# Splits of the first quad and of wo's first data moved ahead, and ScalarE's order within a slot changed

## The reference

```python
# cond: linear layer plus a low-rank adapter chosen per sequence
base_out = jnp.einsum('bti,oi->bto', x, W) + b
lora_h = jnp.einsum('bti,bir->btr', x, lora_As[adapter_mapping])
c = base_out + jnp.einsum('btr,bro->bto', lora_h, lora_Bs[adapter_mapping]) * 2.0
# attention: 32 query heads on 8 key/value heads of 128, rotary positions, causal
q, k, v = _rope(c @ wq), _rope(c @ wk), c @ wv
attn = softmax(where(allowed, q @ k.T * sm_scale, neg))
x1 = x + (attn @ v) @ wo
# cond2: linear layer plus rank-16 experts, two best of 8 by router logits with a language bias
# ffn: linear layer plus rank-64 experts, two best of 16 by a softmax router; float32 output
```

## Time and profile before

| what | value |
|---|---|
| median of 3 runs | 2829.83 us (2829.41 to 2833.12) |
| the profiled execution's own time | 2826.46 us |
| its span in the profile | 2824.5 us |
| PE busy | 2701.7 us, 96% |
| POOL busy | 1198.7 us, 42% |
| DVE busy | 1344.0 us, 48% |
| ACT busy | 854.5 us, 30% |
| mean granted clock of PE | 0.986 |

### The profile page before, as it was taken

One profiled execution on the slowest core, in us unless ns is written; L12 is line 12 of the kernel. 1 busy time (PEld: TensorE's weight loads), 2 busy tenths in 40 slices (PEclk: granted clock), 3 DMA queues, 4 the chain that ended last, 5 costly groups with the idle time before them and its releaser, 6 DMA issues.

```text
span 2824.5 us, 37498 instructions
## 1 busy us (share of the span) xinstructions
PE 2701.7 (96%) x14520; PEld 2174.1 (77%) x14520; DVE 1344.0 (48%) x2011; ACT 854.5 (30%) x2089; POOL 1198.7 (42%) x790
## 2 busy tenths in 40 slices
PE   8979899999998999999998989999999899999999
PEld 7857677777776788887877767777777678888877
DVE  2124667777775111124533557777777511112452
ACT  2222244444443312221212224444444331121110
POOL 0025665655665245510304476566555434441020
PEclk9999999999999999999999989999999999999999
DMA  6853122222225333111543312222222433311322
GB/s 217 243 145 119 45 68 73 70 75 68 71 62 189 126 113 105 51 39 54 145 124 100 109 45 76 75 74 63 67 75 72 168 127 112 105 53 38 84 86 70
DMA packets 311984, 268.47 MB, mean 95 GB/s; under 512 B 68218, under 2 KB 283386, under 8 KB 311810
## 3 DMA queue, kind: packets, MB, share of 16 engines
q1 hardware_dynamic: 250210, 210.50, 24.6%
q10 hardware_dynamic: 61600, 55.58, 6.0%
HBM read 201.88 MB, written 64.16 MB: 94 GB/s over the span
## 4 chain that ended last, share of the span: by engine, by line
PE 85%; POOL 6%; ACT 3%; DMA 2%; issue 2%; SPq 1%; DVE 1%; ACTq 0%; POOLq 0%
PE prod L658 25%; PE prod L660 24%; PE prod L659 24%; PE turned L901 3%; PE turned L851 2%; POOL s_lo L1465 2%; POOL o_lo L1499 1%; ACT probs L1227 1%; ACT s_hi L1213 1%; PE turned L652 1%; PE turned L884 1%; PE prod L1086 1%; POOL w_sum L1489 1%; PE prod L766 1%; POOL w_lo L1430 1%
## 5 line engine op out<-in xcount | busy, mean ns | idle before, releaser
L1430 POOL TENSOR_TENSOR w_lo<-raw,w_hi 128x1024 fp32r<-128x1024 f32 x96 | 239.2, 2493 | 850.0 <-ACT w_hi L1146 728.0
L658 PE MATMUL prod<-o_hi,w_hi 128*128 128x512 f32 x1024 | 405.4, 396 | 22.9 <-POOL o_lo L1499 19.2
L659 PE MATMUL prod<-o_lo,w_hi 128*128 128x512 f32 x1024 | 400.8, 391 | 0.0
L660 PE MATMUL prod<-o_hi,w_lo 128*128 128x512 f32 x1024 | 400.4, 391 | 0.0
L1784 DVE TENSOR_TENSOR x<-prod,x 128x512 f32<-128x512 f32 x128 | 88.5, 692 | 603.3 <-PE prod L660 603.3
L1465 POOL TENSOR_TENSOR s_lo<-w_sum,s_hi 128x512 fp32r<-128x512 f32 x192 | 253.0, 1318 | 155.7 <-ACT s_hi L1213 155.7
L658 PE MATMUL prod<-t_hi,s_hi 128*128 128x512 f32 x768 | 312.2, 407 | 3.9 <-POOL s_lo L1465 3.9
L1146 ACT CAST w_hi<-raw 128x1024 fp32r<-128x1024 f32 x128 | 134.1, 1048 | 599.7 <-PE prod L660 428.0
L660 PE MATMUL prod<-t_hi,s_lo 128*128 128x512 f32 x768 | 300.5, 391 | 0.0
L659 PE MATMUL prod<-t_lo,s_hi 128*128 128x512 f32 x768 | 299.8, 390 | 0.0
L658 PE MATMUL prod<-b_hi,s_hi 128*128 128x512 f32 x576 | 239.9, 417 | 15.7 <-POOL s_lo L1465 15.7
(11 more groups left out here) (168 smaller groups left out, 5063.5 us busy)
## 6 DMA issues: line engine op xcount, KB each, us to landing
raw_pair<-in_wq SPq DMA_DIRECT2D x64, 512.0 KB, 4.7
o_scratch<-o_out ACTq DMA_DIRECT2D x64, 512.0 KB, 2.9
raw<-in_wo SPq DMA_DIRECT2D x64, 512.0 KB, 4.0
o_raw<-o_scratch SPq DMA_DIRECT2D x64, 512.0 KB, 7.2
raw<-t_scratch SPq DMA_DIRECT2D x50, 512.0 KB, 3.6
t_scratch<-x ACTq DMA_DIRECT2D x17, 512.0 KB, 4.2
x_raw<-in_x SPq DMA_DIRECT2D x16, 512.0 KB, 5.9
xt_scratch<-x_sum SPq DMA_DIRECT2D x16, 512.0 KB, 3.2
```

The lines of the kernel that those rows point to most:

```text
L658: pe.matmul(dst, wh, xh, start=start, stop=False)
L659: pe.matmul(dst, wh, xl, start=False, stop=False)
L660: return pe.matmul(dst, wl, xh, start=False, stop=stop)
L1430: pool.tensor_tensor(WL[i % 2][:], RAW[i % 2][:], WH[i % 2][:].bitcast(F32), ALU.subtract).then_inc(w_lo, 1)
```

## The change

Several instructions are moved; the arithmetic is the same.

1. `load_a1` of the first half is issued in the fold, ahead of the load for step 6, into a buffer of its own. On ACT and DVE the adapters' cast and subtraction stand behind those of the last four x blocks. For the second half SP issues the adapters behind the loads of W1 tiles 0 and 1; ACT casts tile 0 before the last early x block.
2. ACT casts W1 tile 2 once `h0`, the adapter product, is done, not once `c0` is.
3. `load_pair` loads each quad in two halves with a semaphore each. The first half may land when the last block sum of the quad before is made, the second when its last but one split is. For the first quad of each half of the tokens the halves follow the last two W1 tiles, and ACT casts its first two blocks before the last column of the first layer.
4. In each slot ACT does the attention work first and the cast for the next quad second. PE's second turn of probabilities and its copy on ACT move from slot 0 to slot 1.
5. In the last quad ACT casts wo's tiles 0 and 1 and the first eight pieces of o. POOL subtracts both tiles first, then twelve pieces; DVE subtracts the other four. The mask and exponentials of the tail stand one product earlier.

```diff
+                if i == 6:
+
+                    sp.wait_ge(const_in, 16 * 5)
+                    sp.wait_ge(fold_taken, 4)
+                    load_a1(0)
...
+                for h in range(2):
+                    ks = slice(4 * h, 4 * h + 4)
+                    if g == 0 and qd == 0:
+                        sp.wait_ge(w_lo, pool_no(hf, T_WO - 2 + h) + 1)
+                    elif h == 0:
+                        sp.wait_ge(s_sum, 4 * (n - 1) + 4)
+                    else:
+                        sp.wait_ge(s_lo, 7 * (n - 1) + 6)
...
-                                if at_ == (QD_KV, 0):
+                                if at_ == (QD_KV, 1):
                                     turn_p(gg - 1, 0, 1)
-                                if at_ == (QD_KV, 1):
                                     score(gg - 1, 1, 0)
...
+                for b in range(4, TB):
+                    x_hi(hf, b)
                 act.wait_ge(a_in, 16 * TT * SPT * (hf + 1))
...
-                act.copy(AH[:], AW[:]).then_inc(a_hi, 1)
-                for b in range(4, TB):
-                    x_hi(hf, b)
+                act.copy(AH[:], AWS[hf][:]).then_inc(a_hi, 1)
...
-                for n in range(KC):
+
+                tile_hi(hf, 2, QN["h0"])
+                c_hi(0)
+                for n in range(1, KC):
                     c_hi(n)
                     tile_hi(hf, n + 2, QN[f"c{n}.0"])
...
+                    if j == 3:
+                        s_high(pair_no(hf, 0, 0), 0)
+                        s_high(pair_no(hf, 0, 0), 1)
...
-                            if more and i == 4:
-                                s_high(n + 1, 4)
-                                s_high(n + 1, 3)
-                            elif more and i != 3:
-                                s_high(n + 1, i)
...
+                            if more and i == 4:
+                                s_high(n + 1, 4)
+                                s_high(n + 1, 3)
+                            elif more and i != 3:
+                                s_high(n + 1, i)
+                            if not more:
+
+
+                                if i == 2:
+                                    act.wait_ge(qprod, q_done(last, 1))
+                                    tile_hi(hf, T_WO)
+                                if i == 3:
+                                    act.wait_ge(qprod, q_done(last, 3))
+                                    tile_hi(hf, T_WO + 1)
+                                if i in (5, 6):
+                                    for c in range(4 * (i - 5), 4 * (i - 5) + 4):
+                                        o_high(0, c)
...
                 tile_lo(hf, T_WO)
-                for i in range(KC):
-                    o_low(0, i)
                 tile_lo(hf, T_WO + 1)
-                for i in range(KC, 2 * KC):
+                for i in range(KC + 4):
                     o_low(0, i)
...
+                for c in range(4, KC):
+
+                    dve.wait_ge(o_hi, hf * OKB * 16 + KC + c + 1)
+                    dve.tensor_tensor(chunk_of(o_lows(0), c, 1), chunk_of(o_lows(0, OWP), c, 1),
+                                      OH[0][:, c * TOK + NT:(c + 1) * TOK].bitcast(F32), ALU.subtract
+                                      ).then_inc(o_lo_d, 1)
```

More of the change, by code:

```diff
@@ L144, in build @@
         XS = [sb(f"x_sum{i}", [P, D], offset=(80 + 4 * i) * KB) for i in range(2)]
-        AW = sb("lora_a_raw", [P, TT * D], offset=88 * KB)
+        AWS = [sb(f"lora_a_raw{hf}", [P, TT * D], offset=o * KB) for hf, o in enumerate((188, 88))]
         CR = [sb(f"c_raw{j}", [P, NT], offset=(144 + 2 * j) * KB) for j in range(KC)]
@@ L439, in load_tw, with adapter, load_a1 @@
                 sp.dma_start(dst, src).then_inc(tw_in[n % 4], 16)
+            def adapter(hf, n):
+                return sp.value_load(ID1[0:1, hf * (BATCH // HALVES) + n:hf * (BATCH // HALVES) + n + 1],
+                                     min_val=0, max_val=SLOTS - 1)
+            def load_a1(hf):
+                for n in range(TT * SPT):
+                    t, n8 = n // SPT, n % SPT
+                    m = adapter(hf, n)
+                    sp.dma_start(view(AWS[hf][:, t * D:(t + 1) * D], KC, n8 * RANK1, (n8 + 1) * RANK1),
+                                 A1[bass.ds(m * D, D), :].rearrange("(k p) r -> p k r", p=P)).then_inc(a_in, 16)
             def load_x(hf, b):
@@ L1213, in s_high @@
                     act.copy(view(SH[i][:], 4), src).then_inc(s_hi, 1)
+                for j in range(4):
+                    n = KC + 2 * j
+                    if n + 2 < T_WO:
+                        tile_hi(hf, n + 2, QN[f"c{j}.1"])
+                    if j == 3:
+                        s_high(pair_no(hf, 0, 0), 0)
+                        s_high(pair_no(hf, 0, 0), 1)
+                    q = QN[f"c{j + 4}.1"]
+                    is_prod(q)
+                    xs = slice(j * NT, (j + 1) * NT)
+                    act.activation(CBH["b22"][:, xs], PJ[q % 4][:], ACT.Identity, bias=B1C[:, j + 4:j + 5]
+                                   ).then_inc(cb_hi, 1)
+                    if n + 3 < T_WO:
+                        tile_hi(hf, n + 3, QN[f"c{j + 4}.1"])
+                    for i, (name, src) in enumerate((("t1", CR[j]), ("t3", CE[0]), ("t2", CE[1]), ("t4", CR[j + 4]))):
+                        act.wait_ge(cb_sum, hf * 16 + 4 * j + i + 1)
+                        act.copy(CBH[name][:, xs], src[:]).then_inc(cb_hi, 1)
                 def p1_copy(n):
@@ L1471, in _ @@
                         pool.wait_ge(s_lo, 7 * n)
-                    pool.wait_ge(pair_in, 32 * (n + 1))
+                    for h in range(2):
+                        pool.wait_ge(pair_in[h], pair_count(n))
                     if n == pair_no(hf, 0, 0):
```

119 lines of the change are left out of this document (44 added, 75 removed).

## The result

The changed kernel takes 2805.72 us (median), the kernel before, measured beside it, 2830.9: a ratio of 0.9908, 95% interval 0.9891 to 0.9925. The profiled execution took 2800.71 us (span 2798.7).

What follows compares the result with a forecast made beforehand. PE, busy for 96% of the span, was taken to bound the kernel, so only its idle or slow-clock time counted. Terms -13 + 0 + 9 + 22 + 13 + 24 = 55 us off 2829.83 gave 2775; range 2751 to 2797.

Steps and rivals of the forecast that it cites:

- Place 1: Fold step 6: adapter loads queued ahead of its tile stall PE about 10.6 us, then 2.4 us half clock; -13 us.
- Places 2 and 3: First layer: adapter split late, two new 4.6 us stalls, about 0 net; W1 tile 2 cast earlier removes 3.8 us waits, +9.
- the slow clock: PE at half clock behind long stalls; without this rule the forecast sum would be some 4 us better.
- Place 4: First quads of each half: earlier casts and half-loads cut PE's waits by 11 us per half; +22 us.
- Place 5: Attention first on ACT: 14 waits of 1.35 us go, probs_t waits grow to about 0.8; +13 us.
- Rival (c): Attention: weights second starves POOL, PE waits for s_lo over 3 us per group; 34 us slower, 2864; chance 0.04.
- (b): Attention first on ACT gives nothing: PE waits for probs_t or weights instead; 13 us more, 2788; chance 0.20.
- Place 6: Start of wo: earlier casts and fewer POOL splits bring its second score 12 us sooner per half; +24 us.
- rival (d): Whole kernel: everything at its better bound and the slow clock stretches gone too; 2755; chance 0.09.
- the weaker rule: GpSimd contends with two-input VectorE instructions, so wo's moved subtractions do not free the port: 22 to 24, without it 26.

Runs made afterwards that it cites:

- e3: Changed kernel with the first half's sixteen adapter DMAs spread behind the loads of fold steps 5, 6 and 7, not all ahead of step 6's: 2797.95 us, 0.9870.
- e9: Kernel before plus only attention first in ScalarE's slots, with the second probabilities' turn and copy one slot later: 2817.08 us, 0.9948.
- e8: Changed kernel without the early half load: both halves of each raw_pair wait for the last s split but one: 2785.07 us, 0.9835.
- e11: Changed kernel with the early half load of raw_pair only in the first group of each half: 2783.08 us, 0.9816.
- e13: Changed kernel plus one wait: in later groups GpSimd starts the next pair's sums only after VectorE's first addition of the key and value quad: 2778.69 us, 0.9813.
- e7: Changed kernel with VectorE's four o_lo splits back on GpSimd, which then makes all sixteen: 2810.48 us, 0.9918.

## Why the forecast was wrong

- **Place 1** was right in its mechanism and near its size: 9.87 us of stall, and from an early wait that both kernels share to the first turn of x 12.4 to 14.2 us more in the nine traces. e3 adds that spreading the same load over three steps only moves the push: the x turns still start 8.6 us later than before.
- **Places 2 and 3**: right in mechanism (9.0 us of 9). The stalls of 4.6 us are those forecast, the slow clock behind the first was 0.8 us more. That the sum is exact is partly luck: by the forecast's own terms the halves gain 6.9 and 1.8 us, and they gained 5.8 and 3.2.
- **Place 4**: right where it was reckoned (21.8 of 22). What the forecast did not do was follow the early half load into the 14 later groups. There it hurried GpSimd although nobody waited for it.
- **Place 5 is the step that failed**. Of `probs_t` it says: "PE waited 6.1 / 14 = 0.44 us there and will wait about 0.8. Net 0.95 us x 14 = **+13 us**." With place 5 alone (e9) the wait is 0.85 to 0.89 and the gain 16 us, so the step was sound for the kernel before, though the 0.8 was put down without a working. In the changed kernel the wait is 2.3 us in 11 of 14 groups, with some 1.5 us of slow clock behind 8 of these. The bounds, 0 and 25, were drawn for the place by itself; together with place 4 it came out at -11.8. What the step left out is the overlap of VectorE with GpSimd once place 4 has moved GpSimd's start. e8, e9 and e11 show that it takes place 4's early load, and e13, which leaves the loads alone, that it works through GpSimd's start. That VectorE stands while GpSimd's operation runs, and is not merely slowed, shows in where its sum of `k_rot` ends: 0.54 or 0.55 us behind the end of the operation of GpSimd's that it met, in all 14 slow sums of the kernel before, 15 of the changed kernel and 16 of e13, whether the sum took 0.8 or 1.8 us.
- **Rival (c)** named the two casts behind the exponentials and expected PE to wait for `s_lo`. The casts were late, but it was the copy queued behind them that PE missed. (b) named the right wait, `probs_t`, and put place 5 at nothing; it was a loss.
- **Place 6**: right in its mechanism, 20.3 us of 24. GpSimd's first split came when forecast, but they took 1.47 us each on average where the sum had 1.25, and four given to VectorE are worth 1.4 us per half, not 5 (e7).
- **The range** was narrower than its parts. The better bounds of the six places sum to 89 us and the worse ones to 14, which is 2741 to 2816 us, not the 2755 of rival (d) and the 2797 of the range. And the slow clock costs 2.4 + 2 + 2 us in the forecast's places 1 and 2 but gives 1.7 + 1.4 + 1.4 in places 2 to 4, so that without it the sum would be 1.9 us better, not 4.

The Trainium skill (SBUF — State Buffer, the section on the two separate sides) says that the port pair which VectorE and GpSimd share is an exclusive lock held for a whole instruction, taken by a VectorE operation with two SBUF inputs only against a GpSimd operation that reads SBUF; whichever starts first has it and the other is blocked. The traces agree: VectorE's sum takes 1.61 or 1.18 us behind GpSimd's start against 0.69 to 0.71 ahead of it, with its end tied to GpSimd's, and GpSimd's operation takes 1.61 or 1.74 behind VectorE's against 1.30. The forecast had used the weaker rule, that the two contend, and only at place 6. By the lock, 0.2 us in who starts first decides who stands; here it cost VectorE 0.9 us.

## What to carry to other kernels

Where two engines share a port, an earlier transfer or a removed wait is not free even if nobody waited for it: it moves one engine's operations onto the other's. So follow every moved start into each stage that repeats, and look at the durations of the neighbour (0.69 or 1.6 us), not only at waits. And before an in-order engine's queue is rearranged, ask which entry idles for another engine: the short copy that PE needs next must stand ahead of it, here one moved cast was worth 45 us. Last, an edit's parts can be right one by one and wrong together; test the pair, too.

## What was not expected of the hardware

- A GpSimd wait added to a kernel made it 27 us faster (e13), and loads issued later made it 20 us faster (e8).
- A wait of 2.3 us was followed by a stretch at about half the granted clock in 8 of 11 cases, worth 1.5 us (75.4 against 73.9); none followed the waits of 0.8 to 1.3 us in e8 and e13, whose groups take 71.5 us and the wait. In e11 the waits of 3.2, 3.2 and 2.15 us were followed by one, the wait of 2.10 in e8 and that of 1.77 in e9 were not. Why some were spared stays open.
- Sixteen adapter loads on one queue took 18.2 us in the fold, 26.7 when spread over three steps of it (e3), 17.6 behind the x blocks and 24.2 ahead of the last of them. What makes two of these slower was not tried.
- A sum of `k_rot` that starts while GpSimd is at work ends 0.54 or 0.55 us behind GpSimd's operation, in 45 of 45 slow sums of three traces. GpSimd's operation that starts during such a sum ends 1.13 to 1.16 us behind it, in 12 of 12 of the changed kernel, e8 and e9.
